# Where the dispatch buffer is filled, and which engine scales the first batch's input

## The reference

```
x = x + L0_xattn(_layernorm(x), ctx)      # the part that the change is in
x = x + L0_moe(_layernorm(x))             # top 2 of 8 experts, capacity 640 rows each
x = x + L1_xattn(_layernorm(x), ctx)
x = x + L1_moe(_layernorm(x))             # top 2 of 8 experts
```

```
y  = clip(ln_out / in_scale, -448, 448);  xq = fp8(bf16(y))
q  = einsum(xq * in_scale, wq) * w_scale
```

## Time and profile before

| | |
|---|---|
| runs | 3048.16 us median (3046.93 to 3048.58) |
| the profiled execution | 3051.39 us, of which the span of the trace is 3049.6 |
| PE busy | 2834.9 us, 93% of the span |
| DVE, ACT, POOL busy | 59%, 56%, 57% |
| mean granted clock of PE | 0.973 |
| `layer0_attention` | its last matmul of the output projection starts at 1112.4 us |
| fill of `disp` | 4 DMAs of 2605 KB, issued from 117.4 us |

### The profile page before, as it was taken

The page is one execution under the profiler, slowest core; times in us unless marked ns, Lnnn a source line. Parts: engine busy times, 40 slices in busy tenths (PEclk is TensorE's granted clock), DMA queues, the critical chain, the costliest instruction groups (busy, mean ns, idle before and its releaser), DMA issues. The chain is left out here.

```text
span 3049.6 us, 57678 instructions
## 1 busy us (share of the span) xinstructions
PE 2834.9 (93%) x16353; PEld 1636.1 (54%) x16354; DVE 1807.4 (59%) x5590; ACT 1703.4 (56%) x4562; POOL 1749.1 (57%) x2443
## 2 busy tenths in 40 slices
PE   4699999999999969999999999959999999985998
PEld 2366666666666644555555555424555555543664
DVE  4366666666666646433443444539989988863443
ACT  5578777787777742332332333427777777751332
POOL 6467777777777624544453544447677777731222
PEclk9899999999999989999999999979999999998999
DMA  7711121111211145544554454735665555557444
GB/s 244 257 43 50 56 80 59 49 49 56 80 59 49 46 142 166 158 136 138 161 154 135 139 159 136 215 76 114 122 137 132 118 131 129 127 108 292 83 81 68
DMA packets 467530, 360.90 MB, mean 118 GB/s; under 512 B 295521, under 2 KB 366305, under 8 KB 467425
## 3 DMA queue, kind: packets, MB, share of 16 engines
q1 hardware_dynamic: 404912, 282.85, 32.5%
q0 software_dynamic: 16496, 37.79, 6.2%
q10 hardware_dynamic: 46016, 38.99, 4.4%
HBM read 186.23 MB, written 110.39 MB: 97 GB/s over the span
## 5 line engine op out<-in xcount | busy, mean ns | idle before, releaser
L1393 POOL TENSOR_TENSOR e_st<-e_st,e_ws_tile 128x1024 f32<-128x1024 f32 x64 | 123.9, 1936 | 429.0 <-PE e_y L1149 417.3
L752 ACT ACTIVATE a_nrm<-a_mm,a_sc_t 128x128 f32<-128x128 f32 x768 | 290.9, 475 | 123.5 <-POOL a_sc_t L905 123.3
L603 DVE BATCH_NORM_STATS2 a_st<-a_mm 128x6 f32<-128x128 f32 x768 | 170.5, 284 | 290.5 <-PE a_mm L440 208.0
L439 PE MATMUL a_mm<-a_w_hi,a_xq_hi 128*128 128x512 f16 x768 | 296.9, 387 | 23.3 <-POOL a_xq_lo L887 15.1
L1187 ACT ACTIVATE e_hh<-e_ha 128x512 f16<-128x512 f32 x128 | 76.3, 596 | 413.3 <-PE e_ha L1134 412.0
L440 PE MATMUL a_mm<-a_w_hi,a_xq_lo 128*128 128x512 f16 x768 | 297.0, 387 | 0.0
L1282 DVE SCALAR_TENSOR_TENSOR e_hl<-e_ha,e_hh 128x512 f16<-128x512 f32 x128 | 88.4, 691 | 351.7 <-ACT e_hh L1187 351.3
L904 POOL TENSOR_TENSOR a_sc_t<-a_sc_t,a_mhalf 128x4 f32<-128x4 f32 x192 | 204.1, 1063 | 118.5 <-DVE a_sc_t L610 118.2
L1148 PE MATMUL e_y<-e_w2l,e_hh 128*128 128x512 f16 x640 | 242.6, 379 | 0.0
L1147 PE MATMUL e_y<-e_w2h,e_hh 128*128 128x512 f16 x640 | 242.6, 379 | 0.0
L1149 PE MATMUL e_y<-e_w2h,e_hl 128*128 128x512 f16 x640 | 242.6, 379 | 0.0
(11 more groups left out here) (366 smaller groups left out, 8221.4 us busy)
## 6 DMA issues: line engine op xcount, KB each, us to landing
e_st<-in_w SPq DMA_DIRECT2D x128, 512.0 KB, 4.1
disp<-a_empty SPq DMA_DIRECT2D x16, 2084.0 KB, 8.0
e_st<-in_w1b SPq DMA_DIRECT2D x32, 352.0 KB, 3.1
disp<-a_empty SPq DMA_DIRECT2D x4, 2605.0 KB, 21.5
e_xb<-disp SPq DMA_DIRECT2D x40, 260.5 KB, 4.3
e_xb<-disp ACTq DMA_DIRECT2D x40, 260.5 KB, 2.7
a_cx<-in_ctxT SPq DMA_DIRECT2D x32, 256.0 KB, 3.3
a_stage<-in_wprojT SPq DMA_DIRECT2D x16, 512.0 KB, 4.9
```

What stands on the lines that cost most here:

```text
L439: pe.matmul(out, xq_hi[:, n, c, :], w_hi[:, t, c, :], start=(c == 0), stop=False)
L752: ins = act.activation(nrm[:, n % 2, i * P:(i + 1) * P], src[:, i * P:(i + 1) * P], ACT.Identity, bias=sc_t[:, n % 2, 3, i:i + 1], scale=s ...
```

## The change

Two edits, both in `layer0_attention`.

- The four fills of `disp` in slot 15 of batch 0 become eight of half the size each. They are in a new stage `fill_disp`, last in SP's plan, and run in slots 0, 2, 4, ..., 14 of batch 1. The scatter waits for eight.
- For batch 0 alone, `x_scaled` and `x_high` leave POOL. ACT gets a new stage `x_split` for each set, at the offsets that `x_scaled` had (10, 12, 14, 16): four activations of 128x128 (a scale for each block of features) that write `xqs`, and, after a wait for these, one copy of 128x512 that writes `xq_hi`. POOL's `x_low` waits for that copy. `x_split` waits for `xq_ok` of the set before, since `xqs` has one buffer. At offset 16 `ctx_split` comes ahead of it in ACT's plan.

```diff
--- before.py
+++ after.py
@@ -269,7 +269,7 @@
 
         sem = {n: s.sem(n) for n in (
             "small", "ready", "wconv_act", "wconv_pool", "wconv_dve", "wx_hi", "gchain", "dchain", "achain",
-            "x_in", "c_in", "x_stat", "x_scal", "x_norm", "x_tr", "x_t", "y_act", "y_pool", "xq", "xq_ok", "cx_hi", "cx_lo",
+            "x_in", "c_in", "x_stat", "x_scal", "x_norm", "x_tr", "x_t", "y_act", "y_pool", "xq", "xq_scaled", "xq_split", "xq_ok", "cx_hi", "cx_lo",
             "mm", "stat", "scal", "norm", "v_ok", "qtr", "q_ok",
             "score", "max", "exp", "rinv", "pnorm", "ptr", "p_ok", "pv", "oy", "cq", "proj",
             "xres", "x1", "out", "filled", "disp_filled", "rconst", "r_stat", "r_scal", "r_norm", "r_tr", "r_t",
@@ -373,9 +373,12 @@
                     for dst, src in ((table, I["route_consts"]), (upper32, I["upper"]),
                                      (wg, I["Wg"].rearrange("p (k e) -> p k e", e=E))):
                         sp.dma_start(dst, src).then_inc(sem["rconst"], 16)
-                    for n in range(4):
-                        sp.dma_start(disp[n * TILES // 4 * P:(n + 1) * TILES // 4 * P, :].rearrange("(c p) d -> p c d", p=P),
-                                     empty[:].unsqueeze(1).to_broadcast([P, TILES // 4, RW])).then_inc(sem["disp_filled"], 16)
+
+            def fill_disp(b, t):
+                if isinstance(b, int) and b == 1 and t % 2 == 0:
+                    lo, hi = (n * TILES // (NJ // 2) for n in (t // 2, t // 2 + 1))
+                    sp.dma_start(disp[lo * P:hi * P, :].rearrange("(c p) d -> p c d", p=P),
+                                 empty[:].unsqueeze(1).to_broadcast([P, hi - lo, RW])).then_inc(sem["disp_filled"], 16)
 
             def residual(b, a):
                 if a == 5:
@@ -390,8 +393,8 @@
                     sp.dma_start(dst[bass.ds(b * FILL * P, FILL * P), :].rearrange("(c p) d -> p c d", c=FILL),
                                  empty[:].unsqueeze(1).to_broadcast([P, FILL, RW])).then_inc(sem["filled"], 16)
 
-            run_pipeline(sp, [("job", 0, lambda b, t: weights(b, t + 1)), ("att", 5, residual), ("end", 10, store), ("in", 1, x_load)],
-                         NJ, SCORE_AT, head=HEAD)
+            run_pipeline(sp, [("job", 0, lambda b, t: weights(b, t + 1)), ("att", 5, residual), ("end", 10, store), ("in", 1, x_load),
+                              ("job", 0, fill_disp)], NJ, SCORE_AT, head=HEAD)
             sp.wait_ge(sem["out"], 16 * (B + 1))
             for dst in spare:
                 sp.dma_start(dst, empty[:, 0:dst.shape[1]]).then_inc(sem["filled"], 16)
@@ -722,6 +725,21 @@
                                              bias=bsc[:, SCALE_OF[n], c:c + 1], scale=wsc[:, SCALE_OF[n], c:c + 1])
                 ins.then_inc(sem["y_act"], 1)
 
+            def x_split_of(n):
+                def x_split(b, k):
+
+                    if not (isinstance(b, int) and b == 0):
+                        return
+                    act.wait_ge(sem["xq"], n // 2 + 1)
+                    if n:
+                        act.wait_ge(sem["xq_ok"], n)
+                    for c in range(KT):
+                        ins = act.activation(xqs[:, c, :], xq[:, n, c, :], ACT.Copy, scale=isc[:, SCALE_OF[n], c:c + 1])
+                    ins.then_inc(sem["xq_scaled"], 1)
+                    act.wait_ge(sem["xq_scaled"], n + 1)
+                    act.activation(xq_hi[:, n, :, :], xqs[:], ACT.Copy).then_inc(sem["xq_split"], 1)
+                return x_split
+
             def ctx_split(b, k):
                 act.wait_ge(sem["c_in"], 16 * (b + 1))
                 if not (isinstance(b, int) and b == 0):
@@ -818,7 +836,8 @@
             run_pipeline(act, [("in", 5, convert_at(-4)), ("in", 7, convert_at(-3)), ("in", 9, convert_at(-2)),
                                ("in", 9, convert_at(-1)), ("job", 3, q_keep), ("att", 1, exps), ("job", 1, normalise), ("job", 0, convert),
                                ("att", 3, p_keep), ("job", 1, v_keep), ("in", 4, x_norm), ("in", 6, x_back),
-                               ("in", 8, y_part), ("in", NJ, ctx_split), ("end", 12, r_norm), ("end", 14, r_keep),
+                               ("in", 8, y_part), ("in", NJ, ctx_split),
+                               *(("in", X_QUANT_AT[n // 2] + 2 * (n % 2) + 1, x_split_of(n)) for n in range(4)), ("end", 12, r_norm), ("end", 14, r_keep),
                                ("end", 17, r_exp)], NJ, SCORE_AT, head=HEAD)
 
         @block.gpsimd
@@ -866,6 +885,8 @@
             def x_scaled_of(n):
                 def x_scaled(b, k):
 
+                    if isinstance(b, int) and b == 0:
+                        return
                     pool.wait_ge(sem["xq"], at(n // 2, 2, b))
                     if not (isinstance(b, int) and b == 0 and n == 0):
                         pool.wait_ge(sem["xq_ok"], at(n - 1, 4, b))
@@ -875,15 +896,19 @@
             def x_high_of(n):
                 def x_high(b, k):
 
-                    if not (isinstance(b, int) and b == 0):
-                        last_use = max(t for t, name in enumerate(JOBS) if name[:-1] == SETS[n])
-                        pool.wait_ge(sem["mm"], at(last_use, NJ, b - 1))
+                    if isinstance(b, int) and b == 0:
+                        return
+                    last_use = max(t for t, name in enumerate(JOBS) if name[:-1] == SETS[n])
+                    pool.wait_ge(sem["mm"], at(last_use, NJ, b - 1))
                     ch.add(pool.tensor_tensor(xq_hi[:, n, :, :], xq[:, n, :, :], in_scale(n), ALU.mult))
                 return x_high
 
             def x_low_of(n):
                 def x_low(b, k):
-                    ch.wait()
+                    if isinstance(b, int) and b == 0:
+                        pool.wait_ge(sem["xq_split"], n + 1)
+                    else:
+                        ch.wait()
                     pool.tensor_tensor(xq_lo[:, n, :, :], xqs[:], xq_hi[:, n, :, :], ALU.subtract)\
                         .then_inc(sem["xq_ok"], 1)
                 return x_low
@@ -920,7 +945,7 @@
 
             def r_scatter(b, k):
                 pool.wait_ge(sem["r_slot"], b + 1)
-                pool.wait_ge(sem["disp_filled"], 16 * 4)
+                pool.wait_ge(sem["disp_filled"], 16 * (NJ // 2))
                 ch.link(pool.tensor_tensor(rsl[:, 0:1], mone[:, 0:1], mone[:, 0:1], ALU.mult))
                 for n in range(2):
                     pool.indirect_dma_start(
```

## The result

The changed kernel takes 3025.26 us (3024.93 to 3025.98, 4 runs) against 3047.55 us (4 runs): a ratio of 0.9923, 95% interval [0.9908, 0.9937], or 22.3 us less (the interval is 19 to 28 us). The forecast was 21.2 us less. Measured again beside other variants, it took 3026.81 us against 3048.20 (0.9933 [0.9919, 0.9946]). Two executions far outside all others, one of before at 7902 us and one of the variant "ctx_split ahead" at 6109 us, are left out of every median; the latter is the only one that was profiled in that variant's second run, and no more is read from it than one start time at 46 us.

What follows compares the result with a forecast made beforehand. TensorE (PE), busy 93% of the span, was taken as the bound, with time to be had where it idles or runs at low clock. -19.8 - 2.4 + 1.0 = -21.2 us takes the median from 3048.16 to 3027.0 us; range 3021 to 3034.

Steps and rivals of the forecast that it cites:

- Part 1, the wait for x: Batch 1's start: with the fill in eight parts, DVE's wait for batch 2's x goes whole, -19.8 us.
- C: SP's queue: x still sits behind the whole fill; no gain, +1 us, 3049 us; chance 0.04.
- A: Without DVE's wait for x another wait shows, so half the gain comes back: 3038 us; chance 0.08.
- The low clock: PE after its restart at 158.24 us: work at granted clock 0.54 runs at full clock, -2.4 us, at most 2.65.
- D: Layer 0 attention: without the rest PE runs at clock 0.94, not 1.00; slower, 3084 us; chance 0.02.
- Fills beside busy engines: From 122 to about 148 us the fill's parts run beside busy engines; cost 0.
- Part 2: Prologue: first batch's quantised input on ScalarE moves POOL's second `scales`, +1.0 us, bounds -1.6 and +3.
- B: First batch runs late as KX0's conversion moves 15.4 us and holds weight buffers: +5 instead of +1, 3031 us; chance 0.06.
- The two signs that I gave: Batch 0's preparation: POOL's second `scales` at 43 to 45 us, and set 3's low half ending at 39.

Runs made afterwards that it cites:

- ctx_split ahead: The changed kernel with ACT's ctx_split of batch 0 moved ahead of the third set's split (offset 13): 3022.59 us against 3048.20 before, 0.9920.
- two buffers: The changed kernel with ctx_split moved ahead, plus a second buffer (xn) for batch 0's scaled input: 3020.36 us against 3045.68 before, 0.9916.

## Why the prediction was right, step by step

**Part 1, the wait for x: right in place and mechanism.** x leaves at 118.84 us, 2.7 us earlier than I had it as all before it is earlier, and no wait over 4 us stands anywhere from 125 to 160 us. The rivals for it are answered: C by the timeline of SP; A by PE at 19.95 and 20.00 us of 20. The size of the term was taken from one execution. The same wait was 17.1, 17.5, 18.5 and 18.6 us in four other kernels that have it, so 19.8 was its upper end, and the mean of the five, 18.3 us, is the better figure. xres landed at 131.4 us, where I had 133 and had left x and ctx out of what stands ahead of it.

**The low clock: right, -2.6 us where I took -2.4.** The bound of 2.65 us, worked out from busy time and granted clock, was met: 42.9, 43.4 and 43.6 us from x_stats to the final sum in the three profiles with the cold restart, 40.8 us in every profile without the gap and in the one with the gap itself filled. D falls: the clock is 1.00 from 140 to 300 us without the rest.

**Fills beside busy engines: right, 0.** PE is at full pace while the fill runs (120 to 140 us, DMA share 1.03).

**Part 2: the term that was mis-sized, and with the wrong sign.** I had +1.0 us; it is -1.5 in the profile of after, and -1.7 in both other profiles that hold the edit as it is. No median shows it: the edit alone is 0.7 us below before, within the noise. B falls, as the milestones of after lose nothing from 49 to 95 us. Two inputs were off.
- ACT's four activations take 1.28 us, not 1.6. My row, L721 in the earlier trace rows, has a scale and a bias by pointer, these only a scale. The Trainium skill (ScalarE: Activation LUTs, What ACT_TABLE_LOAD costs) says that each pointer operand adds some 93 ns; 3.17 / 8 = 0.40 against 1.28 / 4 = 0.32 us agrees, though the two rows differ in their types too. Over four sets and their hand-overs the last low half starts at 36.39 us, where I had 37.85.
- The pair of wx_lo takes 2.47 us, not the 4.16 that I gave some weight. They still hold each other up there, but POOL loses this time: its first `scales` step takes 2.01 us where it took 1.02. ACT's first norm waits 1.65 us for that one, but has time to spare: before the second norm ACT waits again, 0.42 us, for the second `scales`. POOL's second `scales` starts at 41.39 us, below both of my 43.2 and 45.0: the chain in front of it was 1.5 us shorter, and most of the contention fell on an instruction with slack.

The two signs that I gave were missed with it: POOL's second `scales` not at 43 to 45 us but at 41.39, set 3's low half ending at 37.5, not 39. What I had right of part 2 is its shape: the second `scales` is what counts, ctx_split has moved into the way, ACT and POOL alternate over one buffer. The variants with ctx_split ahead and with two buffers show that these two were worth 2.7 us each.

**The rest of the difference.** Between the two roundings before took 29.57 us. All variants have the same instructions there; ten other profiles show 28.3 to 28.8, that with two buffers 29.5. So some 0.9 us of the 2.75 at 126 us is most likely chance in the one profile, not the change. With the better figures the sum of the forecast's terms is 18.3 + 2.6 + 1.6 = 22.5 us, and the medians differ by 22.3; as the interval is 19 to 28 us, that agreement says little. That the forecast of 21.2 us came so near is in part luck: the wait was taken 1.5 us too large and part 2 was 2.6 us off the other way. The profiles differ by 26.1 us, as the profiled execution of before was 3.8 us above the median of its four runs (3.2 above the one that the prediction used). What is left open: behind the last projection the same code takes 1930.6 to 1939.0 us in the twelve profiles. That is more than part 2 is worth, and no experiment here bears on it.

## What to carry to other kernels

A small load that the pipeline needs next should not be issued behind a large fill on the same queue: put the load ahead, or on another queue. Here four whole fills behind the load did as well as eight parts around it. Where PE is the bound, a gap of it costs its length and, behind it, the difference of the two clock levels over the work until the clock returns, and both can be read from windows before the change. When two engines pass a single buffer to and fro, look at a second buffer and at the order of the side jobs in their lists: here each was worth 2.7 us in the profiles, and moving two of the three passes to the other engine 1.5.

## What the runs showed of the hardware

- SP's issue of a 256 KB load took 8.23 us behind four fills of 2605 KB and 0.33 us with none ahead (four fills behind x); behind the four, SP's next issue came only at 141.10 us, when that one had ended.
- A load on ScalarE's queue landed in 6.9 us while another queue filled the DMA engines (share 1.00 and 354 GB/s from 117 to 125 us), ahead of a fill issued 0.9 us before it.
- After 20 us of rest PE ran 5.8 us at a granted 0.54; kept at work with throw-away matmuls it came out of the same gap at 1.00, 2.6 us earlier.
- DVE with two SBUF inputs beside POOL: the pair took 2.36 us alone. Beside POOL it took 4.16 us and cost two POOL instructions some 2 us together, 3.32 us (with two buffers) or 2.47 us, each of these with 1.0 us on POOL's `scales`. So either engine, or both, can lose.
